# Who makes the gate product in the mixture of experts, and three casts fewer or elsewhere in the attention projections

## The reference, cut to what matters

```python
gate = silu(x @ gate_proj[e]);  up = x @ up_proj[e]
out += weight[token, e] * ((gate * up) @ down_proj[e])
```

## Time and profile before

| what | value |
|---|---|
| median of 3 runs | 2651.7 us (2651.52 to 2652.37) |
| profiled execution | 2660.67 us, its span 2658.6 us |
| VectorE busy | 1832.5 us (69% of the span) |
| TensorE busy | 2099.5 us (79%) |
| ScalarE busy | 1346.9 us (51%) |
| GpSimd busy | 583.0 us (22%) |
| `hb` on GpSimd | 64 instructions, 2296 ns each |
| mixture's experts | about 638 to 1106 us of the span |
| projections | about 1121 to 1152, 1488 to 1525, 2364 to 2412 us |

### The profile page before, as it was taken

The page is one execution under the profiler, slowest core; times in us unless marked ns, Lnnn a source line. Parts: engine busy times, 40 slices in busy tenths (PEclk is TensorE's granted clock), DMA queues, the critical chain, the costliest instruction groups (busy, mean ns, idle before and its releaser), DMA issues. The chain is left out here.

```text
span 2658.6 us, 35498 instructions
## 1 busy us (share of the span) xinstructions
PE 2099.5 (79%) x11529; PEld 1344.7 (51%) x11529; DVE 1832.5 (69%) x3840; ACT 1346.9 (51%) x2550; POOL 583.0 (22%) x689
## 2 busy tenths in 40 slices
PE   5999999975675566487586689567999999966978
PEld 3676676753332233255365335345667676742545
DVE  5877788765999899874588686548334353558835
ACT  4666666545887788534433336532434333341651
POOL 2332233312554454210253100111101010101000
PEclk8999999987666766578678779768999999985989
DMA  5000000001110210040320210023000000014000
GB/s 194 1 3 3 2 3 1 1 11 58 42 42 3 76 40 27 25 140 5 70 59 7 69 46 3 17 75 154 2 2 0 1 0 2 1 60 98 27 34 16
DMA packets 62766, 94.49 MB, mean 36 GB/s; under 512 B 9787, under 2 KB 56459, under 8 KB 60023
## 3 DMA queue, kind: packets, MB, share of 16 engines
q1 hardware_dynamic: 59340, 87.81, 10.6%
q0 software_dynamic: 1728, 4.22, 0.7%
q10 hardware_dynamic: 1536, 0.49, 0.1%
HBM read 80.53 MB, written 10.49 MB: 34 GB/s over the span
## 5 line engine op out<-in xcount | busy, mean ns | idle before, releaser
L1250 DVE SCALAR_TENSOR_TENSOR moe_acc<-moee_eo,moee_wt,moe_acc 128x256 f32<-128x256 bf16 x512 | 229.6, 514 | 0.3
L761 DVE SCALAR_TENSOR_TENSOR l_acc<-l_px,l0w_chan,l_acc 128x253 f32<-128x253 f32 (+2 forms) x288 | 137.5, 477 | 100.0 <-POOL l_acc L729 99.4
L1163 POOL TENSOR_TENSOR moee_hb<-moee_gb,moee_ub 96x1024 bf16<-96x1024 bf16 x64 | 146.9, 2296 | 228.3 <-DVE moee_gb L1257 228.3
L1176 PE MATMUL moee_pu<-moe_xb,moee_wb 128*96 128x512 bf16 x256 | 101.1, 537 | 100.6 <-DVE moee_ub L1232 100.6
L1212 ACT CAST moee_eo<-moee_po 128x512 bf16<-128x512 f32 x224 | 115.3, 594 | 80.6 <-PE moee_po L1187 80.6
L1187 PE MATMUL moee_po<-moee_db,moee_hb 96*128 96x256 bf16 x512 | 110.5, 389 | 45.0 <-DVE moee_eo L1241 27.5
L1176 PE MATMUL moee_pg<-moe_xb,moee_wb 128*96 128x512 bf16 x256 | 100.7, 536 | 34.0 <-POOL moee_db L1148 24.0
L3012 DVE SCALAR_TENSOR_TENSOR l3b_sz<-l3b_sig,l3b_pz 128x256 f32<-128x256 f32 x48 | 20.2, 421 | 142.3 <-ACT l3b_sig L2990 142.3
L350 PE MATMUL ln_pt<-ident,xn 128*128 128x128 f32 x176 | 40.6, 424 | 98.3 <-DVE xn L281 98.3
L1176 PEld LDWEIGHTS moee_pu<-moe_xb,moee_wb 128*96 128x96 bf16 x256 | 35.1, 161 | 163.9 <-DVE moee_ub L1232 141.6
L1662 ACT ACTIVATE l3xa_ex<-l3xa_pS 128x512 f32<-128x512 f32 x128 | 74.1, 605 | 85.9 <-PE l3xa_pS L1575 81.5
(11 more groups left out here) (623 smaller groups left out, 5894.8 us busy)
## 6 DMA issues: line engine op xcount, KB each, us to landing
moee_wf<-in_moe_up SPq DMA_DIRECT2D x64, 192.0 KB, 2.4
l3w_w_in<-in_l_w_in SPq DMA_DIRECT2D x1, 8224.0 KB, 26.0
m1b_bc<-bc_rows SPq DMA_DIRECT2D x16, 512.0 KB, 6.2
l0w_w_in<-in_l_w_in SPq DMA_DIRECT2D x1, 6448.0 KB
moee_df<-in_moe_down SPq DMA_DIRECT2D x64, 96.0 KB, 2.1
l_qs<-parts_q SPq DMA_DIRECT2D x36, 128.0 KB
l0w_w_out<-in_l_w_out SPq DMA_DIRECT2D x1, 3072.0 KB
parts_q<-l_pieces SPq DMA_DIRECT2D x16, 192.0 KB, 2.5
```

The costliest lines, as they stand in the source:

```text
L761: nc.vector.scalar_tensor_tensor(out=a, in0=px[:, 0:S - (L0_CONV - 1 - c)], scalar=w, in1=a, op0=ALU.mult, op1=ALU.add).then_inc(tap_done, 1)
L1163: nc.gpsimd.tensor_tensor(hb[:, e % 3, :], gb[:, e % 4, :], ub[:, e % 4, :], ALU.mult).then_inc(h_done, 1)
L1176: last = nc.tensor.matmul(ps[0:MOE_F, half, :], wb[:, e % R, k, n * MOE_F:(n + 1) * MOE_F], xb[:, k, half * 512:(half + 1) * 512], start=( ...
L1250: last = nc.vector.scalar_tensor_tensor(out=acc[:, t, :], in0=eo[:, i % 2, t, :], scalar=wt[:, i, t:t + 1], in1=acc[:, t, :], op0=ALU.mult ...
```

## The change

In the mixture the product `hb` moves from GpSimd's list to VectorE's, right behind the product into `gb`. GpSimd keeps only the casts of weights. In the projections the third cast goes: the second subtraction writes its result as bf16. With a rotation, ScalarE makes the first part (a cast from float32), and VectorE splits unit u-1 after it has rotated unit u. ScalarE's clears move to the end of each step.

```diff
@@ mixture, GpSimd
-                    for e in range(U):
-                        if e + 3 < U:
-                            cast_weights(e + 3)
-                        pool.wait_ge(gated, e + 1)
-                        pool.wait_ge(u_read, e + 1)
-                        if e >= 3:
-                            pool.wait_ge(o_done, e - 2)
-                        nc.gpsimd.tensor_tensor(hb[:, e % 3, :], gb[:, e % 4, :], ub[:, e % 4, :],
-                                                ALU.mult).then_inc(h_done, 1)
+                    for e in range(3, U):
+                        cast_weights(e)
@@ mixture, VectorE, behind the product into gb
+                            dve.wait_ge(gated, i + 1)
+                            dve.wait_ge(u_read, i + 1)
+                            if i >= 3:
+                                dve.wait_ge(o_done, i - 2)
+                            nc.vector.tensor_tensor(hb[:, i % 3, :], gb[:, i % 4, :], ub[:, i % 4, :],
+                                                    ALU.mult).then_inc(h_done, 1)
@@ projections, ScalarE, step u (the clear now stands last in the step)
+                        if rotary:
+                            act.wait_ge(rotated, u + 1)
+                            if u >= 2:
+                                act.wait_ge(sent[u % 2], 32 * (u // 2))
+                            nc.scalar.copy(parts[0:width, u % 2, 0, :], qf[0:width, u % 2, :]).then_inc(first_done, 1)
@@ projections, VectorE
+                def rotate(u):
...
+                    dve.wait_ge(proj, u + 1)
+                    if u >= 1:
+                        dve.wait_ge(rotated, u)
...
+                    nc.vector.tensor_tensor(now, now, t1[0:width, :], ALU.add).then_inc(rotated, 1)
+                def split(u):
...
+                    if not rotary:
+                        nc.vector.tensor_copy(part[0], now).then_inc(first_done, 1)
+                        dve.wait_ge(first_done, u + 1)
+                    link(nc.vector.tensor_tensor(r, now, part[0], ALU.subtract))
+                    link(nc.vector.tensor_copy(part[1], r))
+                    nc.vector.tensor_tensor(part[2], r, part[1], ALU.subtract).then_inc(split_done, 1)
+
+                for u in range(len(units) + rotary):
+                    if rotary and u < len(units):
+                        rotate(u)
+                    if u >= rotary:
+                        split(u - rotary)
```

More of the change, by code:

```diff
@@ L1277 @@
 PAIRS = ((0, 0), (0, 1), (1, 0), (1, 1), (0, 2), (2, 0))
[L1280 to L1286, removed]
 def head_parts(parts, H, HD):
@@ L1329, in project_heads @@
             "proj", "taken", "qf_done", "split_done", "v_chain", "v_proj", "v_done")
+        rotated, first_done = st.sem("rotated", "first_done")
         cleared, tables_in = st.sem("cleared", "tables_in")
@@ L1365, in _ @@
                 for u in steps:
+                    if u < len(units):
+                        (w, ws, bias, tables, src, out), half = units[u]
+                        width = w.shape[2]
+                        if rotary:
[3 more added lines that the diff above has]
+                            nc.scalar.copy(parts[0:width, u % 2, 0, :], qf[0:width, u % 2, :]).then_inc(first_done, 1)
+                        else:
+                            act.wait_ge(proj, u + 1)
+                            if u >= 2:
+                                act.wait_ge(split_done, u - 1)
+                            nc.scalar.activation(qf[0:width, u % 2, :], pm[0:width, u % 2, :], ACT.Identity,
+                                                 bias=0.0 if bias is None else bias).then_inc(taken, 1)
+                    if u < NT and vb is None:
+                        act.wait_ge(v_proj, u + 1)
+                        nc.scalar.copy(vaug[:, u, :, 0:hd], pv[:, u % 2, 0:heads * hd].rearrange(
+                            "p (h d) -> p h d", d=hd)).then_inc(v_done, 1)
                     if u < len(slots):
@@ L1370, in _ @@
                                              scale=0.0).then_inc(cleared, 1)
[L1371 to L1382, removed]
             @block.gpsimd
@@ L1405, in _, with table, by_s @@
                     dve.wait_ge(tables_in, 16 * len(tables_of))
-                for u, ((w, ws, bias, tables, src, out), half) in enumerate(units):
+                def table(a, width, half):
+                    if a.shape[1] == S:
+                        return a[0:width, None, :].broadcast_to([width, HALF // S, S])
+                    return a[0:width, half * HALF:(half + 1) * HALF].rearrange("p (b s) -> p b s", s=S)
+                def by_s(a):
+                    return a.rearrange("p (b s) -> p b s", s=S)
@@ new lines, in rotate @@
+                    dve.wait_ge(proj, u + 1)
+                    if u >= 1:
+                        dve.wait_ge(rotated, u)
+                    link(nc.vector.tensor_tensor(by_s(t1[0:width, :]), by_s(pm[0:width, u % 2, :]),
+                                                 table(tables[0], width, half), ALU.mult))
+                    nc.vector.tensor_tensor(by_s(now), by_s(pw[0:width, u % 2, :]),
+                                            table(tables[1], width, half), ALU.mult).then_inc(taken, 1)
@@ new lines, in rotate @@
+                    dve.wait_ge(taken, u + 1)
+                    nc.vector.tensor_tensor(now, now, t1[0:width, :], ALU.add).then_inc(rotated, 1)
+                def split(u):
+                    (w, ws, bias, tables, src, out), half = units[u]
+                    width = w.shape[2]
+                    now = qf[0:width, u % 2, :]
+                    r, part = rest[0:width, :], [parts[0:width, u % 2, n, :] for n in range(3)]
+                    if rotary:
+                        dve.wait_ge(first_done, u + 1)
@@ L1426, in _ @@
                     else:
                         dve.wait_ge(taken, u + 1)
+                    if u >= 1:
+                        dve.wait_ge(split_done, u)
                     if u >= 2:
                         dve.wait_ge(sent[u % 2], 32 * (u // 2))
-                    split3(nc, link, now, rest[0:width, :],
-                           [parts[0:width, u % 2, n, :] for n in range(3)]).then_inc(split_done, 1)
+                    if not rotary:
+                        nc.vector.tensor_copy(part[0], now).then_inc(first_done, 1)
+                        dve.wait_ge(first_done, u + 1)
```

## The result

| | before | after |
|---|---|---|
| median of the timed runs | 2651.6 us (2648.85 to 2652.37, 4 runs) | 2617.4 us (2613.97 to 2624.05, 4 runs) |
| profiled execution, its span | 2660.67, 2658.6 us | 2614.23, 2612.4 us |
| VectorE, ScalarE, GpSimd busy | 1832.5, 1346.9, 583.0 us | 1782.5, 1352.0, 453.1 us |

A forecast was written before the change was run, and what follows sets the result against it. VectorE was taken to bound the mixture, busy 100.00 of 100 us. Mixture -28.4 and projections -5.6 us give -34.0: 2626.7 against the profiled 2660.67, or 2617.7 for the median; range 2602 to 2640.

The forecast's parts named there:

- (a): Mixture: the min/add no longer waits for GpSimd's product, its spacing falls from 1.55 to 0.34 us; -33.7 us a turn.
- R4: Mixture, rival: min/add keeps its 1.62 us, not waiting for the product, time 2685; halfway case 2648; 3% each.
- (b): Mixture: the product hb on VectorE adds 0.71 us a step; +20.6 us a turn.
- R2: Mixture, rival: ScalarE keeps its wait for po, 7.0 us a step; only tails and projections gain; time 2638.5; 7%.
- (c): Mixture: GpSimd's remaining weight casts cost VectorE's accumulations 0.39 us a pair in 26 steps; +2.7 us a turn.
- R1: Mixture, rival: a pair of casts costs its whole length, 0.90 instead of 0.39 us; time 2644; 8%.
- R3: Mixture, rival: casts fall beside ub, which reads PSUM, and cost nothing; -10.1 us a turn more, time 2597.5; 13%.
- (d): Tail of a mixture turn: GpSimd's product no longer hits VectorE's accumulations; -3.8 us a turn.
- (e): Lead-in of a mixture turn, steps 0 to 3: ScalarE sets the pace there, so the change is 0.
- Projections: The three projection stages: the third cast goes; -2.1, -1.6 and -1.9 us, together -5.6 us.

The follow-up runs named there:

- small_product: Kernel before, with GpSimd's product cut to 64 of its 1024 columns, the rest of hb zero; 2574.7 us, ratio 0.9708.
- double_hb: Changed kernel in which VectorE makes each product for hb twice, the first into a spare buffer nobody reads; 2656.3 us, ratio 1.0007.
- casts_by_ub: Changed kernel in which GpSimd's weight casts also wait for hb of the expert five back; 2598.8 us, ratio 0.9802.
- after: The changed kernel itself, in its first profile, against the kernel before; median 2617.4 us, ratio 0.9876.
- proj_only: Kernel before with only the new projections, its mixture unchanged; 2643.6 us, ratio 0.9974.
- after_again: The changed kernel run once more, unaltered, as a yardstick; 2618.4 us, ratio 0.9881.
- no_casts: Changed kernel without GpSimd's weight casts from a turn's seventh expert on, old weights used again; 2600.4 us, ratio 0.9791.
- all_three: Changed kernel with casts waiting for an earlier hb, ScalarE's clears first in each projection step, and three buffers for the parts; 2597.4 us, ratio 0.9787.

## Why the prediction was right, and where it wasn't

**(a) The min/add**: right. 412 ns in the median, short in `small_product` too, where only the product shrank. R4 is out.

**(b) `hb` costs 0.71**: right. `gb` then stands 0.71 us ahead of `hb`, and `hb` 0.61 ahead of `ub`; doubled, it costs 0.68. That VectorE alone bounds the step, which R2 denied, is shown by `double_hb` and by 6.55 us a step against R2's 7.0.

**(c) The casts**: the term was mis-sized. I had 0.39 us a pair on every step, 10.1 us a turn. In the steady steps they pay 0.39 in one kind and 0.18 in the other, mean 0.285, which is what they paid before. So the term is 0 and not +2.7 a turn: -5.4 us for both. My text had `po` ending among the accumulations or the two products, and then priced only the first. R1 (0.9 a pair) is out, with groups of 3.64 us and not 4.1. R3 is the kernel `casts_by_ub`: its mechanism is real (the kernel with casts beside `ub` has a mixture only 1.6 us longer than the one without casts, 420.5 against 418.9), but the changed kernel doesn't get there by itself.

**(d) The tails**: right. The last sixteen accumulations of the second turn, against the earlier trace rows:
```profile
1064.84 6.63 DVE L1243 SCALAR_TENSOR_TENSOR moe_acc<-moee_eo,moee_wt,moe_acc 128x256 f32<-128x256 bf16 x16
```
They take 6.63 us instead of 8.29 (6.4 was forecast). From a turn's last `ub` on, 3.4 and 3.3 us are saved; with its own `hb` counted, 3.8 - 0.71 = 3.1 was forecast.

**(e) The lead-in**: wrong, if small; I had put it at 0. The first three steps of a turn got longer by 1.0 us in the first turn and 1.6 in the second. VectorE at the start of the second turn:
```profile
862.74 1.22 DVE L1225 CAST moee_ub<-moee_pu 96x1024 bf16<-96x1024 f32 x1 [1.19 <-PE moee_pu L1169]
...
865.79 0.69 DVE L1250 TENSOR_TENSOR moee_gb<-moee_gb,moee_ex 96x1024 bf16<-96x1024 bf16 x1 [1.49 <-ACT moee_ex L1214]
866.51 0.69 DVE L1256 TENSOR_TENSOR moee_hb<-moee_gb,moee_ub 96x1024 bf16<-96x1024 bf16 x1
867.12 1.21 DVE L1225 CAST moee_ub<-moee_pu 96x1024 bf16<-96x1024 f32 x1
```
ScalarE sets the pace there, as I wrote, but here `hb` stands between its inverse and the next `ub`, so its 0.72 us are on the path, once a turn: in the second turn the next spacing is 4.02 us, as before. A new instruction in a stretch that another engine paces isn't always free if it comes after the wait for that engine. The other 0.8 us of the second turn are not from `hb`. TensorE's granted clock is 0.50 ahead of that turn's first `ub` and 0.67 in the 3 us behind it, where before it was 0.59 and 1.00, and `small_product`, where VectorE makes no `hb`, has a lead-in 1.4 us longer there as well, at 0.50 and 0.69. What the other 0.3 us of the first turn are wasn't settled.

By starts of `ub` the mixture adds up so: steady steps -13.8 and -14.0, lead-ins +1.0 and +1.6, turns' ends -3.4 and -3.3, together -31.9 us. The forecast was 2 x (-33.7 + 19.9 + 2.7) = -22.2, 0 and -6.2. The cast term was 5.4 us too dear, the lead-in 2.6 us too cheap.

**Projections**: right in layer 1; in layer 2 a wait was left out, in layer 3 a wait moved by more than I gave it. The same code gives stages that differ by 3 to 4 us from profile to profile (layer 3: 44.2 to 48.4), so I take means: the new projections stand in six profiles (`after`, `proj_only`, `after_again`, `no_casts`, `casts_by_ub`, `double_hb`), the old ones in three. The last column takes the clock at the start of the stage out, by counting from VectorE's first instruction on: all three old profiles have about half the clock at the start of layers 1 and 2, and of the new ones three in layer 1 and four in layer 2 have the full one.

| | old, mean | new, mean | difference | forecast | difference, from VectorE's first instruction |
|---|---|---|---|---|---|
| layer 1 | 32.3 | 29.9 | -2.4 | -2.1 | -1.6 |
| layer 2 | 37.7 | 37.4 | -0.2 | -1.6 | +1.2 |
| layer 3 | 48.8 | 45.2 | -3.6 | -1.9 | -3.6 |
| sum | | | -6.2 | -5.6 | -4.0 |

So 2.2 of the 6.2 us come from stages that began at a higher clock. I can't say that the change did that: `after` and `after_again` differ in it.

In layer 2 I counted ScalarE's clears onto the end rightly, and that a clear ends the stage is so. The step that failed is my count along ScalarE, which had no wait in it ahead of the last unit's cast: that cast waits for the store of the unit two back, 3.76 us in `after`. In the six profiles this wait is 1.66 to 4.21 us, and the length of the stage less this wait is 33.9 to 34.0 us in the four that began at a clock of 1.00 and 36.3 us in the two at 0.50. At the clock of the kernel before, then, the stage without this wait is 1.4 us shorter than the old 37.7, where -1.6 was forecast, and the wait takes the gain back. GpSimd issues its twelve loads from 1473.71 to 1480.24 us and SP this store from 1474.37 us on, so the loads may be what holds it; that wasn't tried by itself.

In layer 3 units are 3.85 and later 4.3 us apart, as forecast. But the end of the wait for unit 5's store, which I moved by 1.5 us, moved by 3.9:
```profile
2366.81 0.62 ACT L1364 CAST l3x_pieces<-l3xp_qf 128x512 bf16<-128x512 f32 x1 [5.11 <-DMA parts_q<-l3x_pieces]
```
That is 39.45 us into the stage; before it ended 43.39 us into it. In `double_hb`, with the same code, units 6 and 7 wait for 3.81 and 4.08 us, and the gain of the stage is gone. I take it that the store's place among the other transfers decides; what decides that place wasn't settled.

**Total.** 28.4 + 5.6 = 34.0 forecast, 34.2 by the medians, with an interval of 26.5 to 39.2 us. By the stages it is 31.9 + 6.2 = 38.1, or 31.9 + 4.0 = 35.9 without what the clock did at their starts. That the forecast is right to 0.2 us is luck: its errors partly cancel (the gain forecast was 5.4 us too small for the casts and 1.7 for layer 3, and 2.6 too large for the lead-in and 2.8 for layer 2), and the interval is 13 us wide. What held is the main term, the min/add that waited for the product, and the path, VectorE's own list.

## What to carry to other kernels

A VectorE instruction that is far longer than its minimum tells what it waits for by where it ends: look for the GpSimd instruction that ends there, and count the wait as part of what moving that instruction would bring. Then place the GpSimd work that is left beside VectorE's reads of PSUM, with a wait if need be: here this brought another 12 us, more than a third of what the whole change had. And where transfers hold a stage, a saved instruction moves only as much as the next transfer does. Before a gain of 2 us in such a stage is believed, take several profiles and compare those whose stage begins at the same granted clock: here the clock at the start alone was worth 2.2 us.

## What the runs showed of the hardware

- The two casts by GpSimd beside VectorE's cast from PSUM take 0.50 and 0.40 us (`small_product`; 0.65 and 0.39 in the rows of `casts_by_ub`) and cost VectorE next to nothing; the same two beside accumulations take 0.66 and 0.58 us and cost 0.39. Where the first meets the product into `gb` it took 1.45 us, and `gb` lost nothing.
- The first four matmuls of layer 2's projections took 1.96 us at a granted clock of 1.00 and 3.75 us at 0.50, in profiles of the same code, and what followed was 2.2 us later.
- After layer 2 of `all_three` the next stage began 3.4 us after the last instruction of any engine. It began 5.1 to 5.7 us after GpSimd's last issue of loads in the three kernels compared, and in no projection stage less than 5.08 us after it, where it took 0.73 us after a last clear by ScalarE.
- TensorE's granted clock in the mixture (700 to 800 us) went from 0.62 to 0.79 of full speed while its busy time fell from 69 to 63 us of 100; in `small_product` it was 0.89. The shorter step isn't the whole cause: in `double_hb` a step is longer than before (7.25 us) and the clock was 0.73. No gain from it is seen, since VectorE was busy for 99.5 us of the 100.
